# Walking normalised rows, and multiplying the neighbours' sums by their weights per node tile

## The reference

```python
xn = _layernorm(x)
# graph part
neigh_sum  = jax.ops.segment_sum(xn[src], dst, num_segments=6250)
deg        = jax.ops.segment_sum(ones, dst, num_segments=6250)
neigh_mean = neigh_sum / jnp.maximum(deg, 1.0)[:, None]
h   = jnp.concatenate([xn, neigh_mean], axis=-1)
out = jax.nn.relu(h @ W + b)                     # W is 512 x 256
gnn = out / jnp.maximum(norm(out), 1e-12)
# a linear attention over all nodes (4 heads of 32), with rms norms
mix = rmsnorm(linear_attention(rmsnorm(xn)) @ w_out + b_out) + xn
x = x + gnn + mix
# eight experts of hidden size 1024, each node by its best two
xf = _layernorm(x);  logits = xf @ Wr + br
x = x + weighted sum over the two best of  gelu(xe @ W1 + b1) @ W2 + b2
```

## Time and profile before

| | us |
|---|---|
| time, median of 3 runs | 1980.7 |
| span of the profiled execution | 2187.4 |
| first stage | 0 to 89.5 |
| walk | 89.5 to 1307.4 |
| routing | 1307.4 to 1478.4 |
| experts | 1478.4 to 2187.4 |

### The profile page before, as it was taken

How to read it: one execution, slowest core, us unless ns; L and a number is a source line. 1 busy time by engine, 2 the same in 40 slices (tenths; PEclk the granted TensorE clock), 3 DMA queues, 4 the chain that set the end, 5 groups by cost and what they waited for, 6 DMA issues and landing times.

```text
span 2187.4 us, 33907 instructions
## 1 busy us (share of the span) xinstructions
PE 1583.7 (72%) x9422; PEld 1361.2 (62%) x9423; DVE 1101.1 (50%) x3043; ACT 900.9 (41%) x1840; POOL 1140.4 (52%) x1141
## 2 busy tenths in 40 slices
PE   6735536546566667867767763548999999999998
PEld 5524435435454544545545543447999999999997
DVE  6512212212234536655555457765666666666664
ACT  6501101101112323323334336554666666666664
POOL 3267666666656666666666612555333333333333
PEclk9868868767878979988888785558999999999999
DMA  7334333333324655566656526537878777877775
GB/s 210 119 100 114 104 101 107 101 97 103 106 81 154 224 165 182 182 180 184 198 182 189 181 76 197 188 135 248 228 215 220 213 221 208 226 214 221 213 221 137
DMA packets 188123, 368.85 MB, mean 169 GB/s; under 512 B 33324, under 2 KB 134172, under 8 KB 173656
## 3 DMA queue, kind: packets, MB, share of 16 engines
q0 software_dynamic: 77296, 252.50, 41.3%
q1 hardware_dynamic: 102992, 113.64, 16.3%
q10 hardware_dynamic: 7736, 1.52, 0.4%
HBM read 287.94 MB, written 80.39 MB: 168 GB/s over the span
## 4 chain that ended last, share of the span: by engine, by line
PE 50%; another core or an unknown queue 17%; DVE 12%; issue 11%; DMA 5%; ACT 3%; SPq 2%; POOL 0%; DVEq 0%; ACTq 0%; POOLq 0%
PE bank L1813 11%; PE bank L2002 5%; PE bank L2003 5%; PE bank L2004 5%; PE bank L2025 5%; PE bank L2024 5%; PE bank L2026 5%; PE bank L1879 3%; DMA xTs<-xnT_d 3%; PE bank L1830 2%; PE bank L1973 1%; DVE acc_lent L1478 1%; DMA z_d<-w2s_lent 1%; DVE acc_lent L1307 1%
## 5 line engine op out<-in xcount | busy, mean ns | idle before, releaser
L695 POOL DMA_INDIRECT w2s_lent<-z_d,edge_tabs_lent x784 | 777.5, 992 | 438.7 <-issue 256.7
L1307 DVE TENSOR_TENSOR acc_lent<-acc_lent,bank 128x258 f32 x244 | 102.7, 421 | 600.6 <-remote 348.8
L1813 PE MATMUL bank<-w2s_lent,S_lent 128*128 x976 | 261.0, 416 | 19.0 <-issue 9.5
L1031 ACT ACTIVATE G<-bank,acc_lent 128x256 f32<-128x256 f32 x448 | 188.3, 472 | 205.9 <-DVE w2s L1670 124.5
L1813 PE MATMUL bank<-w2s_lent,G 128*128 x976 | 265.9, 422 | 3.4 <-issue 3.4
L2024 PE MATMUL bank<-w2s 128*128 128x256 f32 x896 | 264.4, 295 | 0.0
L2002 PE MATMUL bank<-w2s,acc 128*128 128x256 f32 x896 | 260.4, 291 | 2.8 <-issue 2.8
L739 POOL DMA_INDIRECT out_dram<-G,acc_lent x112 | 179.6, 1604 | 158.3 <-DVE G L1650 117.3
L1629 DVE TENSOR_TENSOR acc<-w1s,acc 128x512 fp32r<-128x512 f32 x224 | 155.1, 693 | 200.7 <-ACT acc L1000 174.1
L2004 PE MATMUL bank<-w2s,acc 128*128 128x256 f32 x896 | 254.0, 284 | 0.0
L2025 PE MATMUL bank<-w2s 128*128 128x256 f32 x896 | 253.7, 283 | 0.4 <-issue 0.4
(11 more groups left out here) (322 smaller groups left out, 2993.3 us busy)
## 6 DMA issues: line engine op xcount, KB each, us to landing
w2s<-w_d POOLq DMA_DIRECT2D x112, 1024.0 KB
w_d<-w2s_lent SPq DMA_DIRECT2D x64, 256.0 KB
acc_lent<-bucket_d SPq DMA_DIRECT2D x56, 266.0 KB
w2s_lent<-z_d,edge_tabs_lent POOLq DMA_INDIRECT x784
bu_d<-w2s_lent SPq DMA_DIRECT2D x98, 128.0 KB
w2s_lent<-bu_d SPq DMA_DIRECT2D x14, 768.0 KB
w1s<-in_L_ffn_W_dram SPq DMA_DIRECT2D x8, 1024.0 KB
w2s_lent<-in_L_ffn_W_dram SPq DMA_DIRECT2D x32, 256.0 KB
```

Of the source, the lines that this page charges most:

```text
L695: pool.indirect_dma_start(out=ring_rows[:, row % (RING * QUAD), 0:D], out_offset=None, in_=z_d[:, :], in_offset=bass.IndirectOffsetOnAxis( ...
L1031: g = act.activation(raw[q % 2][:, k * MT:(k + 1) * MT], bank[q][:, k * MT:(k + 1) * MT], ACT.Gelu, bias=b1c[1 - par][:, 2 * q + k:2 * q + ...
L1307: dve.tensor_tensor(to, to, bank[j % DEPTH][:, 0:ACCW], ALU.add).then_inc(s["acc_done"], 1)
L1813: m = pe.matmul(bank[j % DEPTH][:, 0:ACCW], S_of[j % DEPTH][:, k, :], rows[:, ds(bases[j], ACCW)], start=(k == 0), stop=(k == QUAD - 1))
```

## The change

The first stage normalises and stores the rows themselves, in `xn_d`; the products, their copies and buffers are gone. ACT writes each unit's normalised rows into one of six buffers, POOL stores all 25 units and fills the accumulators with zeros, one piece ahead of each store. PE's work on the edge tables stands in a row without the units between. The walk gathers from `xn_d`. `w_neigh` is loaded by SP in the walk, behind `M2_ready`, instead of by ACT at the start.

In routing the sums of a tile are turned on PE (`agg_turn`), copied by ACT (`r_aggT`), multiplied by `w_neigh` (`agg_out`, into banks 7 and 4 by turns), and `r_y` reads the product from PSUM. All turned sums go through bank 3. Relu, payload, turn and copies now count by pairs of tiles (`PAIRS_OF`) instead of by three. The `follow` matmuls in routing are left out. POOL's load of the first expert's second weights and PE's first turn of the experts wait for the last y.

```diff
-LN_BUFS = 3
+LN_BUFS = 6
...
+            def store_xn(n):
                 t0, nt = tiles_of(n)
-                z_taken(pool, n)
-                pool.dma_start(z_t[:, t0:t0 + nt, :], zs[n % LN_BUFS][:, 0:nt, :]).then_inc(z_out[n % LN_BUFS], 16)
+                a = zero_acc(n)
+                if n == LN_UNITS - 1:
+                    a.then_inc(s["acc_zeroed"], 1)
+                pool.wait_ge(s["xn_ready"], n + 1)
+                pool.dma_start(xn_t[:, t0:t0 + nt, :], xn[n % LN_BUFS][:, 0:nt, :]).then_inc(xn_out[n % LN_BUFS], 16)
...
-                    pool.indirect_dma_start(out=ring_rows[:, row % (RING * QUAD), 0:D], out_offset=None, in_=z_d[:, :],
+                    pool.indirect_dma_start(out=ring_rows[:, row % (RING * QUAD), 0:D], out_offset=None, in_=xn_d[:, :],
...
             sp.wait_ge(s["M2_ready"], 1)
+            sp.dma_start(w_neigh, gnn_W[D:2 * D, :].rearrange("(c p) n -> p c n", p=P)).then_inc(s["neigh_in"], 16)
...
             def unit_xn(n):
                 t0, nt = tiles_of(n)
                 act.wait_ge(s["ln_ready"], n + 1)
-                until(act, s["xnT_mm"], n + 1 - LN_BUFS)
+                xn_free(act, n)
...
             def ln_step(n):
                 if n + 1 < LN_UNITS:
                     unit_sd(n + 1)
-                if n < LN_UNITS:
-                    unit_xn(n)
-                if 1 <= n <= LN_UNITS:
-                    unit_xnT(n - 1)
-                if n >= 3 and n % 2:
-                    unit_z(n - 3)
-                if ZEROS_FIRST <= n < LN_UNITS:
-                    a = zero_acc(n)
-                    if n == LN_UNITS - 1:
-                        a.then_inc(s["acc_zeroed"], 1)
+                unit_xn(n)
...
+            def r_aggT(g):
+
+                for k, (tt, n) in enumerate(PAIRS_OF[g]):
+                    act.wait_ge(s["aggT_mm"], PAIRS_BEFORE[g] + k + 1)
+                    until(act, s["agg_mm"], PAIRS_BEFORE[g])
+                    act.activation(aggT[:, tt:tt + n, :], bank[3][:, 0:n * D].rearrange("p (t d) -> p t d", d=D),
+                                   ACT.Copy).then_inc(s["aggT_ready"], 1)
...
+            act.wait_ge(s["qu_evac"], NT)
+            r_aggT(0)
             r_relu(0)
             for g in range(GROUPS):
+                if g + 1 < GROUPS:
+                    r_aggT(g + 1)
                 r_sd(g)
...
             def r_y(g):
                 t0, nt = GROUP_AT[g], GROUP_LEN[g]
                 dve.wait_ge(pair["u_in"][g % 2], 16 * (g // 2 + 1))
...
+                for k, (first, n) in enumerate(PAIRS_OF[g]):
+                    at = PAIRS_BEFORE[g] + k
+                    dve.wait_ge(s["agg_mm"], at + 1)
+                    for j in range(n):
+                        tt = first + j
+                        a = dve.scalar_tensor_tensor(out=acc[:, t0 + tt, 0:D], in0=agg_bank[at % 2][:, j * D:(j + 1) * D],
+                                                     scalar=rdeg[:, t0 + tt:t0 + tt + 1], in1=ub_of[g][0][:, tt, :],
+                                                     op0=ALU.mult, op1=ALU.add)
+                    a.then_inc(s["y_ready"], 1)
...
+            def agg_turn(g, k):
+
+                first, n = PAIRS_OF[g][k]
+                until(pe, s["aggT_ready"], PAIRS_BEFORE[g] + k)
+                for j in range(n):
+                    for c in range(DC):
+                        m = pe.transpose(bank[3][:, j * D + c * P:j * D + (c + 1) * P],
+                                         acc[:, GROUP_AT[g] + first + j, c * P:(c + 1) * P], ident[:, :])
+                m.then_inc(s["aggT_mm"], 1)
+
+            def agg_out(g, k):
+
+                first, n = PAIRS_OF[g][k]
+                at = PAIRS_BEFORE[g] + k
+                pe.wait_ge(s["aggT_ready"], at + 1)
+                until(pe, s["y_ready"], at - 1)
+                for j in range(n):
+                    for c in range(DC):
+                        m = pe.matmul(agg_bank[at % 2][:, j * D:(j + 1) * D], aggT[:, first + j, c * P:(c + 1) * P], w_neigh[:, c, :],
+                                      start=(c == 0), stop=(c == DC - 1))
+                m.then_inc(s["agg_mm"], 1)
+
+            def r_agg(g):
+                pairs = len(PAIRS_OF[g])
+                agg_turn(g, 0)
+                for k in range(1, pairs):
+                    agg_turn(g, k)
+                    agg_out(g, k - 1)
+                agg_out(g, pairs - 1)
...
+            pe.wait_ge(s["neigh_in"], 16)
+            pe.wait_ge(s["qu_evac"], NT)
+            pe.wait_ge(s["o_evac"], NT)
+            r_agg(0)
             for g in range(GROUPS):
+                if g + 1 < GROUPS:
+                    r_agg(g + 1)
```

More of the change, by code:

```diff
@@ L43 @@
 GROUPS = len(GROUP_AT)
+PAIRS_OF = [[(k, min(2, n - k)) for k in range(0, n, 2)] for n in GROUP_LEN]
+PAIRS_BEFORE = [sum(len(p) for p in PAIRS_OF[:g]) for g in range(len(PAIRS_OF) + 1)]
 ACCW = D + 2
@@ L128, in build_program @@
         edges_d = dram("edges_d", (2, EROWS, P), I32)
-        z_d = dram("z_d", (NT * P, D))
+        xn_d = dram("xn_d", (NT * P, D))
         xnT_d = dram("xnT_d", (NT, P, D))
@@ L379, in build_program @@
         UN = 8
-        z_out = [sem(f"z_out{k}") for k in range(LN_BUFS)]
-        z_sent = [sem(f"z_sent{k}") for k in range(LN_BUFS)]
+        xn_out = [sem(f"xn_out{k}") for k in range(LN_BUFS)]
         def scattered_by(g):
@@ L387, in build_program @@
         W1_FREE = [g for g in range(GROUPS) if GROUP_AT[g] * PAYW < w1_end][-1]
-        def part(it, half):
-            return 2 * it + half if it else 1
         x_t = x[0:(NT - 1) * P, :].rearrange("(t p) d -> p t d", p=P)
-        z_t = z_d.rearrange("(t p) d -> p t d", p=P)
+        xn_t = xn_d.rearrange("(t p) d -> p t d", p=P)
         bu_t = bu_d.rearrange("t p d -> p t d")
@@ L844, in _ @@
             a.then_inc(s["kv_weights"], 1)
-            for n in range(LN_STEPS, LN_UNITS + 3):
+            for n in range(LN_STEPS, LN_UNITS):
                 ln_step(n)
@@ L956, in r_relu @@
                 t0, nt = GROUP_AT[g], GROUP_LEN[g]
-                for first in range(0, nt, 3):
-                    act.wait_ge(s["y_ready"], part(g, first // 3))
-                    y = acc[:, t0 + first:t0 + min(first + 3, nt), 0:D]
+                for k, (tt, n) in enumerate(PAIRS_OF[g]):
+                    act.wait_ge(s["y_ready"], PAIRS_BEFORE[g] + k + 1)
+                    y = acc[:, t0 + tt:t0 + tt + n, 0:D]
                     a = act.activation(y, y, ACT.Relu)
@@ L1558, in _ @@
             dve.memset(picked[:, :, :], 0.0)
-            dve.wait_ge(s["y_ready"], part(1, 1))
+            dve.wait_ge(s["y_ready"], PAIRS_BEFORE[2])
             L.after(dve.memset(padrows, 0.0))
@@ L1922, in r_turn @@
+            def r_agg(g):
[5 more added lines that the diff above has]
+                agg_out(g, pairs - 1)
             def r_turn(g):
                 t0, nt = GROUP_AT[g], GROUP_LEN[g]
-                for half in range((nt + 2) // 3):
-                    pe.wait_ge(s["pay_x"], part(g, half))
-                    for tt in range(3 * half, min(3 * half + 3, nt)):
-                        at = (tt - 3 * half) % 2 * D
+                for k, (first, n) in enumerate(PAIRS_OF[g]):
+                    pe.wait_ge(s["pay_x"], PAIRS_BEFORE[g] + k + 1)
+                    for j in range(n):
@@ L1928, in r_turn @@
                         for c in range(DC):
-                            m = pe.transpose(bank[2 * half + (tt - 3 * half) // 2][:, at + c * P:at + (c + 1) * P],
-                                             acc[:, t0 + tt, c * P:(c + 1) * P], ident[:, :])
+                            m = pe.transpose(bank[k][:, j * D + c * P:j * D + (c + 1) * P],
+                                             acc[:, t0 + first + j, c * P:(c + 1) * P], ident[:, :])
                     m.then_inc(s["xT_mm"], 1)
-                    follow()
@@ L1934, in r_logits @@
             def r_logits(g):
                 nt = GROUP_LEN[g]
-                for half in range((nt + 2) // 3):
-                    pe.wait_ge(s["xT_ready"], part(g, half))
-                    for tt in range(3 * half, min(3 * half + 3, nt)):
+                for k, (first, n) in enumerate(PAIRS_OF[g]):
+                    pe.wait_ge(s["xT_ready"], PAIRS_BEFORE[g] + k + 1)
+                    for tt in range(first, first + n):
                         for c in range(DC):
```

166 lines of the change are left out of this document (41 added, 125 removed).

## The result

| | before | after |
|---|---|---|
| time, median, us | 1981.02 (4 runs) | 2027.05 (4 runs) |
| ratio | | 1.0226, interval 1.0199 to 1.0252 |
| span of the profiled execution, us | 2187.4, and 1972.8 in a second one | 2026.2 |

The change makes the kernel slower by 46 us; 2020 was forecast, in a range from 1977 to 2052.

A forecast was written before the change was run, and what follows sets the result against it. The first stage (DVE's way) and routing (DVE nearly the bound, then a loop without overlap) were to decide. First stage -22.5, weights 0, cycles +52, head +10: +39.5 us, scaled +36; forecast 2020 us, range 1977 to 2052.

The forecast's parts named there:

- the loop's terms: Routing cycle: projection, last pair of y, y to payload, payload to logits; 10.6 + 1.05 + 5.0 + 9.5 = 26.1 us against 18.3.
- the projection: Routing cycle: PE turns and projects group g+1 behind the logits of g-1, with ACT's copies in between; 10.6 us.
- y to payload: Routing cycle: from the end of y through relu, squares and table load to the payload; 4.9 us, 5.0 with e2.
- payload to logits: Routing cycle: six scalings, the last turn and the logits; 9.5 us with hand-over, 7.0 with faster turn and logits.
- The rival that the clock rises throughout: Routing: projections keep TensorE at 2.4 GHz, cycles take 21.4 us, 1983 us or 1974 in all; chance 0.20.
- -22.5: First stage: without projections and copies of z the gathers start near 67 us, 22.5 us sooner; range -31.5 to -11.5.
- The 2 us put for the landing of the last rows: End of first stage: the last normalised rows land in an estimated 2 us, against 10.65 for an early block.
- the 65.0 us of DVE's way: First stage: 89.5 us less 8.3 and 16.2 leaves DVE 65.0 us, all its other idle time kept.
- The rival that landings hold the buffers back: First stage: store landings of 10.65 us hold the six buffers, gathers start at 78, 2031 us; chance 0.08.
- The head: Start of routing: later x1 and payload of group 0 cost +8 to +12.4 us, taken as +10.
- the landing of the output rows: Head of routing: payload of group 0 also waits for output rows, 9.57 us to land, ending by 1335.7.
- Where hiding was assumed: Weights load taken as 0; POOL's zeroing and stores, 35 to 51 us, hidden under 67; walk unchanged.

The follow-up runs named there:

- the fill: Changed kernel plus unread matmuls in PE's idle times of each routing cycle, 36 and 12 (2029.61 us), then 72 and 32 (2020.66 us); 0.84 and 0.92 belong to the larger.
- the opened loop: Changed kernel with the projection one group earlier and the orders of ACT, DVE and the head of routing refitted: 1971.52 us, ratio to before 0.9957.
- the second profile of before: The kernel before, unchanged, profiled again: span 1972.8 us, walk 1036 us, routing cycles of 15.2 us.

## Why the prediction was right, and where it was off

**The routing cycle.** The mechanism was right: the payload of g waits for the projection of g+1, and the logits for that payload. Leaving the projection out took the growth away; shifting it by one round took most of it (17.0), and with the other orders fitted all of it (14.7). The difference of 7.8 us a cycle measured 8.6. Both levels were too high, though, 26.1 and 18.3 where 23.8 and 15.2 were measured; that 2.3 and 3.1 us of error nearly cancel in the difference is luck. The 18.3 came from the long execution. That its span stood 206.7 us over the median was on the table in front of me, and I added the difference as it was instead of asking in which stage it lay; rows 7 were such rows. Of the loop's terms, the projection took 9.0 to 10.9 us, 9.9 in the mean (10.6 forecast), and y to payload 4.9 (5.0); payload to logits took 9.1 in the cycle shown (9.5), 7.1 in the one before it, where the logits ran in 3.08, and 8.4 in the mean of six.

**The clock.** The rival that the clock rises throughout did not come: 0.67 was granted, logits ran at 3.1 us in some cycles and 5.1 in others. The rival's cycle of 21.4 us was sized well: the two cycles with the fill at 0.92 took 21.3. Its price of 4.7 us was not, since the loop stood at 23.8 and not at 26.1: about 2.5 us. The clock also rose with the order of the work: 0.82 once PE no longer stood waiting in the loop, with no fill at all. The Trainium skill ("TensorE: Matmul & The Clock Gate", section What's actually happening) has activity release the throttle; the granted clocks of these runs agree (0.67, 0.84 with the fill, 0.82 in the opened loop).

**The first stage.** -22.5 was forecast and -15.7 measured. The 2 us put for the landing of the last rows were right:

```profile
74.51 1.03 POOL L684 DMA_INDIRECT w2s_lent<-xn_d,edge_tabs_lent  x1 [2.21 <-DMA xn_d<-w2s_lent]
```

The step that failed is the 65.0 us of DVE's way ahead of it, with "all its other idle time kept": the last store was issued only at 72.3. Of the 74.5 us DVE now waits 8.1 for loads, where before it waited for none; its own work measures 57.0, where 61.4 less 8.3 leaves 53.1; and the rest of its idle time is 9.4, where 11.9 was kept. That the loads had passed under the copies of z is the inference named above. The rival that landings hold the buffers back did occur, as 12.7 us of ACT's waiting, but with eight buffers that went and the gather stayed, so it was beside the path.

**The head.** +10 was forecast, +5.3 measured. x1 of group 0 began 18.4 us after the last sum, near what was worked out (19 to 21). The term that failed is the landing of the output rows, 9.57 us by the earlier trace rows:

```profile
out_dram<-acc_lent SPq DMA_DIRECT2D x1, 384.0 KB, 2.5
```

They landed in 2.5 us, issued at 1131.4, with the DMA engines at a share of 0.46 meanwhile; in the second profile of before they took 9.5, at a share of 1.03. So nobody waited for them: ACT went from `r_relu(1)` straight into the payload at 1136.56, 25.3 us after the last sum, where 28 to 32.7 were worked out.

**Where hiding was assumed.** The load of the weights, POOL's zeroing and its stores cost nothing: POOL was busy 42.8 of 74.5 us, within the 35 to 51 worked out. The walk was unchanged at 1036 us. What lies behind the last cycle, +2.8 us, was put at 0.

## What to carry to other kernels

When work is moved from a place where it is hidden to a place that is nearly full, look in each engine's order for what it is put ahead of: here 9 to 11 us of PE work in each cycle closed a loop through PE, DVE and ACT, and the seven cycles cost 60 us. One round earlier, and with the other engines' orders fitted to it, the cycles were as short as without that work, and some 9 us of it were left in the kernel's time. Order every engine so that what it does next already has its input, and only then count busy time. And before a profile is summed, lay its span beside the median, and if they differ find the stage in which they do.

## What the runs showed of the chip

One profiled execution of the same kernel took 2187 us, 177 of the extra between the first gather and the last sum (1213.4 against 1036.3 us), spread over the walk, with the gathers' own number and size unchanged; what caused it no run here shows. Filling PE's pauses raised the granted clock from 0.67 to 0.84 and took 0.9 us off a cycle of 23.8, and 2.5 where 0.92 was granted; a better order raised it to 0.82 by itself. The same store of 384 KB landed in 9.5 us while the DMA engines were at a share of 1.03, and in 2.5 us at 0.46.
